# A transformer block on one core: attention and feed-forward stages in one block without a barrier, the residual added as the output is evicted

## The reference

```python
# x: (4, 1024, 512), t: (4, 128), 16 heads of 32, hidden size 2048, all float32
def _L0_cond_ref(x, t, ...):
    x = x + _attention(_tc_rmsnorm(x, t, g1w, g1b, b1w, b1b), Wq, Wk, Wv, Wo)
    return x + _swiglu(_tc_rmsnorm(x, t, g2w, g2b, b2w, b2b), gate_w, hid_w, out_w)
return x + _L0_cond_ref(x, cond_256, ...)
```

## Time and profile before

| what | value |
|---|---|
| median of 3 runs | 2409.89 us (2408.28 to 2412.3) |
| the profiled execution, its whole time | 2412.49 us |
| its span, first to last instruction | 2410.4 us |
| busy PE / DVE / ACT / POOL | 95% / 69% / 54% / 59% |
| mean granted TensorE clock | 0.983 |
| last matmul of the attention stage ends | 1384.28 us |
| first product of the feed-forward stage starts | 1427.64 us |

### The profile page before, as it was taken

One profiled execution on the slowest core, in us unless ns is written; L12 is line 12 of the kernel. 1 busy time (PEld: TensorE's weight loads), 2 busy tenths in 40 slices (PEclk: granted clock), 3 DMA queues, 4 the chain that ended last, 5 costly groups with the idle time before them and its releaser, 6 DMA issues. The chain is left out here.

```text
span 2410.4 us, 40369 instructions
## 1 busy us (share of the span) xinstructions
PE 2284.6 (95%) x10916; PEld 1570.9 (65%) x10916; DVE 1666.5 (69%) x2740; ACT 1310.2 (54%) x2335; POOL 1424.3 (59%) x1329
## 2 busy tenths in 40 slices
PE   5999999999999999999999849999999999999999
PEld 4655447555466554475554538888888888888887
DVE  4777735776637777357766358877887788778877
ACT  3367772567753677725677444454435444544454
POOL 0399980799943998908989437603770267127611
PEclk9999999999999999999999969999999999999999
DMA  5222212221132222122221422136312631253125
GB/s 189 78 58 51 64 41 85 71 53 44 50 107 53 61 50 62 41 85 71 54 45 49 161 91 98 36 102 202 117 36 92 196 124 44 88 192 132 44 83 179
DMA packets 92656, 209.60 MB, mean 87 GB/s; under 512 B 15632, under 2 KB 15632, under 8 KB 90640
## 3 DMA queue, kind: packets, MB, share of 16 engines
q1 hardware_dynamic: 90768, 194.32, 27.1%
q10 hardware_dynamic: 576, 8.39, 0.9%
q0 software_dynamic: 1088, 4.19, 0.5%
HBM read 134.23 MB, written 19.92 MB: 64 GB/s over the span
## 5 line engine op out<-in xcount | busy, mean ns | idle before, releaser
L732 DVE TENSOR_REDUCE pmax<-bank 128x1 f32<-128x512 f32 x1024 | 652.8, 684 | 203.9 <-PE bank L974 193.9
L644 ACT ACTIVATE probs<-bank 128x512 f32<-128x512 f32 x1024 | 567.2, 602 | 288.2 <-PE bank L1077 232.0
L479 POOL TENSOR_TENSOR sums<-sums,probs 128x512 f32<-128x512 f32 x432 | 540.9, 1287 | 0.0
L1077 PE MATMUL bank<-qs,ks 128*128 128x512 f32 x1024 | 435.8, 429 | 14.1 <-ACT probs L644 11.4
L974 PE MATMUL bank<-ks,qs 96*128 96x512 f32 x1024 | 407.4, 410 | 31.2 <-DVE pmax L732 30.1
L1077 PEld LDWEIGHTS bank<-qs,ks 128*128 128x128 f32 x1024 | 192.9, 189 | 274.9 <-issue 124.4
L1637 PE MATMUL bank<-H_hi,wt_hi 128*128 128x512 f32 x896 | 350.0, 391 | 14.7 <-DVE H_lo L1492 14.6
L1651 PE MATMUL bank<-ow,aw 128*128 128x512 f32 x1536 | 358.6, 392 | 0.0
L1637 PE MATMUL bank<-H_lo,wt_hi 128*128 128x512 f32 x896 | 349.5, 390 | 0.0
L1637 PE MATMUL bank<-H_hi,wt_lo 128*128 128x512 f32 x896 | 349.5, 390 | 0.0
L1651 PEld LDWEIGHTS bank<-ow,aw 128*128 128x128 f32 x1536 | 285.7, 188 | 59.7 <-issue 1.2
(11 more groups left out here) (156 smaller groups left out, 3385.0 us busy)
## 6 DMA issues: line engine op xcount, KB each, us to landing
raw<-in_gu_w SPq DMA_DIRECT2D x66, 512.0 KB, 3.5
wo_raw<-in_out_w SPq DMA_DIRECT2D x128, 256.0 KB, 2.7
ks<-qk_hi SPq DMA_DIRECT2D x136, 128.0 KB, 2.4
qs<-qk_hi SPq DMA_DIRECT2D x264, 64.0 KB, 2.0
x<-in_x SPq DMA_DIRECT2D x10, 1024.0 KB, 5.1
ks<-qk_lo SPq DMA_DIRECT2D x68, 128.0 KB, 2.4
qs<-qk_lo SPq DMA_DIRECT2D x132, 64.0 KB, 2.0
attn_out<-yout SPq DMA_DIRECT2D x32, 256.0 KB, 2.4
```

The costliest lines, as they stand in the source:

```text
L479: nc.gpsimd.tensor_tensor(total, first, probs[:, s % 2, h, :], ALU.add) \
L644: nc.scalar.activation(probs[:, s % 2, h, :], sbank[i % SB][:], ACT.Exp, scale=SCALE).then_inc(st_done, 1)
L732: nc.vector.reduce_max(pmax[:, t, h, hf:hf + 1], mbank[n % MB][:], AX_X).then_inc(sq_done, 1)
L1077: nc.tensor.matmul(sbank[i % SB][:], ks[:, g % 2, h, s * P:(s + 1) * P], qs[:, u % 3, h, :], start=True, stop=True).then_inc(st_ready, 1)
```

## The change

1. Both stages are written into one block, each engine's attention part followed at once by its feed-forward part. In place of the barrier stand explicit waits (`ends`, `wait_for`).
2. The SBUF places of the feed-forward stage are laid anew: the first weights' buffers on Wq and Wk, `x1` on the normalised tokens hT, which are free earlier.
3. The lead of the feed-forward stage is written anew: POOL issues the loads of tokens and first weights behind its last sum of the attention stage, ACT does squares and scaling, POOL the mean, root and `weight_lo(0, 0)`, and transposes, roundings and combinations go through the two column blocks in turn (`FULL_LEAD`, `ROUNDED_LEAD`, `COMBINE_LEAD`). PE waits for each combination before its own product.
4. The residual x is added as an output tile is evicted (`tensor_tensor` in place of a copy), and DRAM gets `x_mid = x + a`. So each batch of attention loads its 8 tiles of x again (`load_residual`, 256 KB each, on SP's queue), and the feed-forward stage loads and adds no x for its norm.
5. In the feed-forward loop ACT rounds the weights of `j = 1` behind the copy of the first product of `j = 0`; some waits of POOL and SP are on other steps.

The core of the diff:

```diff
+    def residual_place(i):
+        return qk[i % 2][:, 1, :].bitcast(F32) if i < 2 or i >= NT - 2 else sums[:, i - 2, :]
...
+        def load_residual(b, i):
+            sp.dma_start(residual_place(i), x[b, i * P:(i + 1) * P, :]).then_inc(residual_loaded[i], 16)
...
+            for s in k_stacked:
+                hold(sp, held, s, b * (NG * HEAD_INC) + (NG + 1) * HEAD_INC)
+            load_residual(b, 0)
+            load_residual(b, 1)
+            hold(sp, held, w_ready, MISC(b, misc_index(True, ("D", NU - 1, 1)) + 1))
+            for t in range(2, NT - 2):
+                load_residual(b, t)
                 for t in range(NT):
                     hold(sp, held, sq_done, SCORES_Q(b, NU * NMAX + t + 1) + MB)
-                    sp.dma_start(attn[b, t * P:(t + 1) * P, :], yout[:, t % 2, :]).then_inc(y_stored[t % 2], 16)
+                sp.dma_start(x_mid[b, t * P:(t + 1) * P, :], yout[:, t % 2, :]).then_inc(y_stored[t % 2], 16)
+                if t < 2:
+                    load_residual(b, NT - 2 + t)
...
-                    nc.vector.tensor_copy(yout[:, t % 2, :], mbank[n % MB][:]).then_inc(sq_done, 1)
+                dve.wait_ge(residual_loaded[t], b * 16 + 16)
+                nc.vector.tensor_tensor(yout[:, t % 2, :], mbank[n % MB][:], residual_place(t), ALU.add).then_inc(sq_done, 1)
...
+FULL_LEAD = [(i, q) for q in range(4) for i in range(2)]
+ROUNDED_LEAD = [(i, slot) for slot in (B11, B21, B22, T2, T1, T3, T4) for i in range(2)]
+COMBINE_LEAD = [(i, slot) for slot in (T1, T2, T3, T4) for i in range(2)]
...
+        wait_for(pool, "projections", "x_mid")
+        load_tokens(0)
+        load_tokens(1)
+        load_raw(0)
+        wait_for(pool, "affine", "norm")
...
+        pool.wait_ge(raw_early[0], 16)
             combos(0, 0, True)
+        wait_for(pool, "wv")
+        load_raw(1)
             combos_lo(0, 0, True)
+        pool.wait_ge(sq_sum, 8)
+        nc.gpsimd.tensor_scalar(var[:], ssq[:], 1.0 / D, EPS, ALU.mult, ALU.add).then_inc(var_ready, 1)
...
             inverse_root(0)
+        weight_lo(0, 0)
+        pool.wait_ge(raw_early[1], 16)
             combos(0, 1)
...
+        wait_for(act, "projections", "exps", "values", "norm")
+        act.wait_ge(raw_early[0], 16)
+        weight_hi(0, 0, True)
             for t in range(8):
                 square(0, t)
+        act.wait_ge(inv_ready, 1)
+        for t in range(8):
+            nc.scalar.activation(x1[:, t, :], x1[:, t, :], ACT.Copy, scale=inv[:, t:t + 1]).then_inc(x_scaled, 1)
+        nc.scalar.activation(ssq[0:1, 0:1], ssq[0:1, 0:1], ACT.Silu)
+        wait_for(act, "stacks", "wv", "split")
+        act.wait_ge(norm_now, 2)
+        for q in range(2):
+            for i in range(2):
+                full_lead(i, q)
+                rounded_lead(i, q)
+        for q in range(2, 4):
             for i in range(2):
+                full_lead(i, q)
+        for slot in (B22, T2, T1, T3, T4):
+            for i in range(2):
+                rounded_lead(i, slot)
...
-                if j < NJ - 1:
+                if 0 < j < NJ - 1:
                         weight_hi(b, j + 1, False, (0, 1))
                     act.wait_ge(prod_done, b * (NP * NJ) + NP * j + 1)
                     nc.scalar.activation(a[:, j, 0, :], psum[4 * (j % 2)][:], ACT.Copy).then_inc(p1_copied, 1)
+                if j == 0:
+                    weight_hi(b, 1, False, (0, 1))
```

More of the change, by code:

```diff
@@ new lines, in attention_program @@
+    wo_stored = sem("wo_stored")
+    x_loaded = sem("x_loaded")
+    wv_loaded = sem("wv_loaded")
+    wo_loaded = sem("wo_loaded")
+    st_ready = sem("st_ready")
+    st_done = sem("st_done")
+    sq_ready = sem("sq_ready")
+    sq_done = sem("sq_done")
+    w_ready = sem("w_ready")
+    w_act = sem("w_act")
+    w_dve = sem("w_dve")
+    full = sem("h_full")
+    q_stacked = [sem(f"q_stacked{h}") for h in range(GH)]
+    k_stacked = [sem(f"k_stacked{h}") for h in range(GH)]
+    m_rows = sem("m_rows")
@@ new lines, in attention_program @@
+    pv_done = sem("pv_done")
+    sum_done = sem("sum_done")
+    mt_ready = sem("mt_ready")
+    od_act = sem("od_act")
+    den_ready = sem("den_ready")
+    den_up = sem("den_up")
+    o_up = sem("o_up")
+    residual_loaded = [sem(f"residual_loaded{i}") for i in range(NT)]
+    on_done = sem("on_done")
+    os_act = sem("os_act")
+    os_dve = sem("os_dve")
+    y_stored = [sem("y_stored0"), sem("y_stored1")]
+    sq_sum = sem("sq_sum")
+    var_ready = sem("var_ready")
+    inv_ready = sem("inv_ready")
@@ new lines, in lo_part @@
+                    tokens = mspare[:].rearrange("p (g c) -> p g c", g=NG)
+                nc.vector.tensor_tensor(osplit[:, t % 2, 1, :, :], tokens,
+                                        osplit[:, t % 2, 0, :, :].bitcast(F32), ALU.subtract).then_inc(os_dve, 1)
+            for q in range(NT * KT):
+                for n in range(sum(MAX_IN_V[:q]), sum(MAX_IN_V[:q + 1])):
+                    max_tile(b, n)
+                tile = IN_V.get(q // KT)
+                if q % KT == KT - 1 and tile and tile[0] != "mT":
+                    work_tile(b, tile)
@@ L1100 @@
+    return (sync_part, gpsimd_part, scalar_part, vector_part, tensor_part), ends
 NJ = HID // P
@@ L1120, with ffn_program @@
               9 * i + 8: (i, (T3,)), 9 * i + 9: (i, (T2,)), 9 * i + 10: (i, (T4,))}
-def ffn_program(nc, x, attn, gu_w, out_w, out, cst, psum):
+def ffn_program(nc, ctx, x, x_mid, gu_w, out_w, out, before, cst, psum):
     at = cst["at"]
@@ L1146, in ffn_program, with lead_bank, squares_place, wait_for @@
     mhalf = at("mhalf2", [P, L // P], F32, "mhalf")
-    first, second = psum[0:4], psum[4:8]
+    second = psum[4:8]
+    def lead_bank(i, q):
+        return psum[(0, 1, 2, 3, 6, 7, 4, 5)[4 * i + q]]
+    def squares_place(t):
+        return (hf, ht)[t // 4][:, t % 4, :]
+    def wait_for(engine, *names):
+        for name in names:
+            for semaphore, value in before[name]:
+                engine.wait_ge(semaphore, value)
     def raw_place(j):
@@ new lines, in sem @@
+    def sem(name):
+        return ctx.enter_context(nc.semaphore(name))
+    held = sem("held2")
+    raw_loaded = [sem(f"raw_loaded{i}") for i in range(4)]
+    s_step = sem("s_step")
+    w_hi = sem("w2_hi")
+    w_lo = sem("w2_lo")
+    s_lo = sem("s_lo")
+    prod_done = sem("prod_done")
+    p1_copied = sem("p1_copied")
+    u2_done = sem("u2_done")
+    p5_added = sem("p5_added")
+    c11_done = sem("c11_done")
+    c22_done = sem("c22_done")
+    u3_done = sem("u3_done")
+    c12_done = sem("c12_done")
```

2310 lines of the change are left out of this document (1151 added, 1159 removed).

## The result

| what | before | changed |
|---|---|---|
| median, timed in turn on one chip | 2411.22 us (2408.28 to 2415.37, 5 runs) | 2426.64 us (2425.18 to 2431.11, 5 runs) |
| the profiled execution, its span | 2412.49, 2410.4 us | 2425.18, 2423.4 us |
| mean granted TensorE clock | 0.983 | 0.983 |

The ratio is 1.0067, 95% interval 1.0051 to 1.0083: slower by 15.4 us on the medians. Slower was the likeliest side of the forecast, but the time lies 3.6 us above the range's end.

The account below looks back on a forecast made before the run. PE was taken as busy nearly everywhere, idle mainly at the seam between the stages and the last attention batch end. +21.6 at inner ends, -14.9 at the seam and 0 elsewhere gave +6.7: 2416.6, stated as 2417 us, range 2396 to 2423.

Parts of the forecast that it names:

- +21.6: Three inner attention batch ends: loads of x delay tile 0's store, PE stalls before tile 5; 7.2 us each, +21.6 us.
- the size of the stall: PE before tile 5 at each inner batch end: waits 4.9 us because tile 0's store lands late.
- The clock's 2.7 us: Behind each inner end's stall: PE's granted clock falls to 0.5, costing 2.7 us.
- -14.9: Seam from attention to feed-forward: the lead starts earlier, behind ACT's last osplit; first hidden tile ends 14.9 us sooner.
- the 21.5 given for a tile 5 that isn't delayed: Seam between the stages: if stores and loads don't delay tile 5, the gain is 21.5 us instead of 14.9.
- The rest: 0: Feed-forward loop: removed x work lay beside a busy PE, roundings for j = 1 have cover, loop end unchanged; 0 us.
- The step to the median: Whole kernel: 2419.2 us from the profiled execution becomes 2416.6 on the median, 2.6 lower.
- +6.7: Whole kernel: sum of +21.6 at the inner ends, -14.9 at the seam and 0 for the rest.
- The clock did fall: Inner ends, judging a rival: the clock doesn't fall in the stalls, 2408.5 us; chance 0.12.
- Equal shares of bytes: Batch ends, rival: SP's queue and wv's share equally, store lands at 376.5, stall 2.2 us, 2398 us; chance 0.20.
- Loads ahead of `wv`: Batch ends, rival: SP's four loads precede wv, tile 5 on time, only the seam's -21.5, 2388.5 us; chance 0.12.
- The lead was earlier: Seam, judging a rival: the lead is not earlier, as long as now on ACT, gaining 5 or less, 2426; chance 0.08.

Follow-up runs that it names:

- e14: The changed kernel, unchanged, profiled a second time: one run, 2424.03 us.
- e1: The changed kernel without the loads of x at the attention batch ends, a copy in place of the add at the eviction: 2396.63 us, ratio 0.9939 to before.
- e9: The changed kernel with POOL's combinations of the next batch's first weights two steps of the second projection earlier, SP's waits unchanged: 2423.20 us, ratio 1.0050 to before.
- e13: The kernel before, unchanged, profiled a second time: one run, 2406.66 us.
- e7: The kernel before with wv loaded in eight transfers with rows of 2 KB instead of one with rows of 16 KB: 2415.69 us, ratio 1.0017.
- e8: The changed kernel with wv in 2 KB rows, tile 0's store ahead of the four loads, POOL's combinations earlier but SP's loads delayed: 2412.60 us, ratio 1.0003 to before.
- e5: The changed kernel with SP issuing tile 0's store ahead of the wait for D and the four loads of x: 2414.43 us, ratio 1.0006 to before.
- e4: The changed kernel with wv loaded in eight transfers with rows of 2 KB instead of one with rows of 16 KB: 2414.26 us, ratio 1.0009 to before.
- e6: The changed kernel with POOL's combinations of the next batch two steps earlier, buffers laid so that SP's loads also waited longer: 2434.11 us, ratio 1.0102 to before.
- e10: The changed kernel without the load of wv behind the last batch, which nobody reads: 2423.17 us, ratio 1.0048 to before.

## Why the prediction was right or wrong

**"+21.6" at the inner ends: right in the mechanism, and in the sum only by luck.** The step that failed here is the size of the stall: tile 5's was put at 4.9 us and was 6.27, 6.43 and 6.16. The store landed 13.2 us behind `D`'s end (369.17 to 382.39), not 11.6. All of `wv` and the four loads did come through ahead of it, as taken, but 4.2 MB moved in that time and not 3.41, since 0.7 MB of the transfers behind the store in SP's queue went along, and they moved at some 342 GB/s instead of the 385 of the earlier trace rows. The clock's 2.7 us were 1.7, 2.9 and 2.8: the 36 matmuls of tiles 5 to 7 took 9.63, 10.86 and 10.78 us where 35 x 0.227 is 7.95, and in the windows above the clock is back 3.5 us after the first restart. With 0.4 of old pauses the ends are 7.6, 8.9 and 8.6, together 25.1. The periods say about the same once each is compared with one of before that has the same falls of the clock: 338.59 - 330.8, 338.33 - 328.9 and 337.44 - 328.9 are 7.8, 9.4 and 8.5, together 25.7. The trace of before had a fall in all three periods and that of the changed kernel in one, which took 3.8 of it back and left 21.9. e14, with two falls 45 us ahead of `D` at 2.4 each, gives 7.5, 6.6 and 9.3 in the same way, 23.4: from one execution to the next the ends cost some 23 to 26 us.

**"-14.9" at the seam: mis-sized by 1.9.** The term that failed is the landing of the last end's store, 17.9 us behind `D` and not 16.0: 6.8 MB moved until then and not 6.03, again with 0.7 MB of what stood behind the store, at 377 GB/s over the last 15.4 us. Tile 5 and the lead took 0.3 us more each (5.4 us to ACT's last `osplit` instead of 5.1, 33.1 for the lead instead of 32.8), and the 30 matmuls behind it some 0.7 less. 13.0 remain. e1, where nothing of x is loaded, gains 19.6 against the 21.5 given for a tile 5 that isn't delayed.

**"The rest: 0" failed: +2.5.** The text looked at the roundings of `j = 1` and had the loop's end unchanged. The loop's end is where it went: POOL's waits "on other steps", item 5 of the change, were costed at nothing without a look at what ACT needs from POOL there. In its place the second projection takes 91.8 us instead of 91.16, in every batch. Half of that is shown (e9), the cause of the other half is open.

**The step to the median.** The forecast took 2.6 us off, the distance of the profiled execution of before. Its trace had all three falls of the clock and that of the changed kernel one, so the difference of the spans (13.0) is too small by about 3.8 - 1.55; the terms without luck, 25.7 - 13.0 + 2.5 = 15.2, meet the medians' 15.4, more closely than the 23 to 26 us for the ends allow. Against the forecast's +6.7 these are 4.1 at the ends, 1.9 at the seam and 2.5 in the rest; another 1.3 us of the distance to 2416.6 is that the kernel before has a median of 2411.22 in five runs and 2409.89 in the three that the forecast started from.

**The 1.55 us ahead of D1** belong to no edit: D1 lies between 365.99 and 372.30 in the sixteen traces; e13, the kernel before again, has 365.99 and e7, which differs from it only behind D1, 370.41.

**The rivals.** The clock did fall, in each of the three stalls. Equal shares of bytes would have had the store there 9 us behind `D`; it took 13.2, and 10.7 even with equal packets. Loads ahead of `wv`: no, they land with it (10.5 and 10.0 us). The lead was earlier.

## What to carry to other kernels

Before a transfer is put on a busy queue, count what waits for the next one of that queue, and look at the packets of the other queues as well as at their bytes: cutting `wv` into rows of 2 KB won back 12 us of 15 without changing the bytes. In the kernel before, where PE hardly waited, the same cut cost 4 us. Adding a loaded tile costs DVE no more than the copy did (0.69 us), but the load takes a place in a queue, so it belongs where no store is waited for. And compare periods of a kernel that have the same clock: one trace of before and one of after differed here by 4 us of luck, as much as two of the terms.

## What the runs showed of the hardware

The granted clock fell to its lower level at places where PE only paused for 0.2 to 0.95 us at a time, and not always: in e7, pauses of 0.95 and 0.60 us 45 us ahead of `D` were followed by 0.5, in e8 pauses of 0.95 and 0.59 by 1.00. In the windows of e7, then of e8, behind these pauses:

```profile
1324.00:1325.00 1.00, 1.00 (x9) 0.76 (x13) 0.00 (x0) 1.00 (x3) 1.00 (x2) 0.80 0.00 0
1325.00:1327.50 2.50, 2.50 (x10) 0.77 (x3) 0.00 (x0) 1.30 (x3) 2.50 (x3) 0.50 0.03 7
```

```profile
1328.00:1329.00 1.00, 0.99 (x9) 0.82 (x13) 0.00 (x0) 1.00 (x3) 1.00 (x2) 1.00 0.00 0
1329.00:1331.50 2.50, 2.50 (x19) 0.68 (x17) 0.00 (x0) 2.43 (x4) 2.50 (x3) 1.00 0.02 7
```

Nor does the length of a stall decide it alone. Behind e5's first stall of 2.75 us, and then behind e4's of 3.17 us, 3 us of work each:

```profile
380.00:383.00 3.00, 3.00 (x7) 2.42 (x8) 1.05 (x2) 0.00 (x0) 0.00 (x0) 0.50 0.37 141
```

```profile
380.50:383.50 3.00, 2.94 (x13) 2.48 (x14) 1.46 (x3) 0.00 (x0) 0.00 (x0) 1.00 0.60 227
```

The shorter one cost the clock, in all three inner ends of e5, and the longer one did not, in any of e4 (3.17 and 2.96 us; two waits of 1.12 and 2.24 at the third). The stalls of 5.1 to 6.5 us of the changed kernel, e6, e9, e10 and e14 cost it each time. A price for a stall of about 3 us can be 1.4 us or nothing.

A DVE `tensor_tensor` of 512 columns takes 0.69 us alone and often about 1.2 beside POOL's sums, in both kernels. DVE of the changed kernel while POOL works (1653.22 to 1657.23), and in POOL's wait for ACT behind it (till 1658.40):

```profile
1655.43 1.20 DVE L1573 TENSOR_TENSOR aw<-a,aw 128x512 fp32r<-128x512 f32 x1
...
1657.70 0.68 DVE L1583 TENSOR_TENSOR x<-x 128x512 f32<-128x512 f32 x1
```

The Trainium skill ("GPSIMD Engine Reference", "1. Specifications") has the two engines share their way to SBUF for instructions with two SBUF inputs; the rows agree. An add of the same size with one input in PSUM (`x<-bank,x`) took 0.69 us at 1654.82, in the midst of POOL's sums.
